# Second attention: score products over all 128 rows, with zero rows for the other head of a pair

## The reference

```python
def _L1_attn_ref(x, Wq, Wk, Wv, Wo, bo, w, v):        # h = 16 heads of hd = 16 channels
    q, k, val = (proj(Wq), proj(Wk), proj(Wv))
    R = jnp.abs(pos[:, None] - pos[None, :]).astype(x.dtype)
    R_hat = (1.0 + jnp.exp(vv)) / (1.0 + jnp.exp(vv - wv * R))
    scores = jax.nn.relu(jnp.einsum('bhqd,bhkd->bhqk', q, k)) * R_hat[None]
    scores = jnp.where(causal[None, None], -jnp.inf, scores)
    attn = jax.nn.softmax(scores / np.sqrt(hd).astype(x.dtype), axis=-1)
    ctx = jnp.einsum('bhqk,bhkd->bhqd', attn, val)
    return ctx @ Wo + bo
```

## Time and profile before

| what | value |
|---|---|
| median of 3 runs | 2512.78 us (2505.85 to 2514.34) |
| the profiled execution | 2507.73 us, its span 2505.9 us |
| TensorE busy over the span | 2114.1 us (84%) |
| VectorE, ScalarE, GpSimd busy | 1612.1, 1338.5, 730.1 us |
| mean granted TensorE clock | 0.916 of full speed |
| L2249, score products | 512, from 1590.8 to 2168.2 us of the span |

### The profile page before, as it was taken

The page is one execution under the profiler, slowest core; times in us unless marked ns, Lnnn a source line. Parts: engine busy times, 40 slices in busy tenths (PEclk is TensorE's granted clock), DMA queues, the critical chain, the costliest instruction groups (busy, mean ns, idle before and its releaser), DMA issues. The chain is left out here.

```text
span 2505.9 us, 43979 instructions
## 1 busy us (share of the span) xinstructions
PE 2114.1 (84%) x13087; PEld 1666.7 (67%) x13087; DVE 1612.1 (64%) x4682; ACT 1338.5 (53%) x2662; POOL 730.1 (29%) x837
## 2 busy tenths in 40 slices
PE   3899999999999999868883685588988889888892
PEld 2788888888888888745562463355655556555782
DVE  4666666666666666356764675787877778676335
ACT  2445555555555544335554664587877778711330
POOL 5211111111111111032455565022222212256452
PEclk8999999999999999979986797699999899989896
DMA  6720010000000000023232433422222222152556
GB/s 110 179 35 5 7 34 1 8 11 27 1 8 3 1 1 0 11 81 59 44 61 55 120 98 128 145 81 79 77 73 59 57 78 83 27 149 103 162 168 240
DMA packets 212265, 167.47 MB, mean 67 GB/s; under 512 B 109185, under 2 KB 170161, under 8 KB 212081
## 3 DMA queue, kind: packets, MB, share of 16 engines
q1 hardware_dynamic: 192608, 121.80, 18.5%
q0 software_dynamic: 14240, 38.35, 4.9%
q10 hardware_dynamic: 5232, 5.14, 0.6%
HBM read 91.07 MB, written 74.14 MB: 66 GB/s over the span
## 5 line engine op out<-in xcount | busy, mean ns | idle before, releaser
L633 PE MATMUL psum_o<-w_s,hid_s 128*128 128x256 f32 x3072 | 384.1, 284 | 19.0 <-ACT hid L437 19.0
L619 PE MATMUL psum_h<-xn2T_s,w_s 128*128 128x512 f32 x1536 | 385.7, 401 | 7.0 <-ACT hid L437 3.7
L633 PEld LDWEIGHTS psum_o<-w_s,hid_s 128*128 128x128 f32 x3072 | 371.8, 188 | 26.9 <-issue 19.0
L436 ACT ACTIVATE hid_s<-psum_h,b 128x512 fp32r<-128x512 f32 x256 | 176.5, 690 | 338.9 <-PE psum_h L619 323.4
L619 PEld LDWEIGHTS psum_h<-xn2T_s,w_s 128*128 128x128 f32 x1536 | 283.3, 190 | 84.4 <-ACT hid L437 21.8
L2134 DVE CUSTOM_DVE_ANT_0 ra_z<-ra_psum_s,rhat 128x128 f32<-128x128 f32 (+3 forms) x512 | 228.6, 483 | 85.3 <-PE ra_psum_s L2249 70.8
L2084 ACT ACTIVATE ra_z<-ra_z,ra_nm 128x128 f32<-128x128 f32 (+3 forms) x512 | 244.7, 555 | 0.0
L2013 POOL TENSOR_SCALAR_AFFINE_SELECT ra_z<-ra_z 128x512 f32<-128x512 f32 x128 | 81.6, 637 | 446.8 <-DVE ra_z L2171 446.8
L2261 PE MATMUL ra_psum_p<-ident,ra_z 128*128 128x128 f32 x1280 | 182.7, 294 | 1.0 <-ACT turned L2076 1.0
L2249 PE MATMUL ra_psum_s<-ra_k_st,ra_q_st 48*128 48x128 f32 (+3 forms) x512 | 126.9, 366 | 63.4 <-DVE ra_mx L2134 47.2
L520 DVE TENSOR_TENSOR hid_s<-hid,hid_s 128x1024 fp32r<-128x1024 f32 x128 | 156.0, 1223 | 35.2 <-ACT hid L437 34.3
(11 more groups left out here) (394 smaller groups left out, 4284.0 us busy)
## 6 DMA issues: line engine op xcount, KB each, us to landing
ex_slots<-blank SPq DMA_DIRECT2D x1, 10296.0 KB, 33.9
ex_zT<-ex_slots SPq DMA_DIRECT2D x78, 132.0 KB
ex_rows<-ex_slots SPq DMA_DIRECT2D x8, 1056.0 KB, 9.8
w<-in_L_tok_w SPq DMA_DIRECT2D x8, 1024.0 KB, 6.4
ra_scratch<-ra_hi SPq DMA_DIRECT2D x32, 256.0 KB
ra_scratch<-ra_lo SPq DMA_DIRECT2D x32, 256.0 KB
ra_q_st<-ra_scratch SPq DMA_DIRECT2D x128, 64.0 KB
ra_k_st<-ra_scratch SPq DMA_DIRECT2D x128, 64.0 KB
```

Of the source, the lines that this page charges most:

```text
L436: act.activation(hid_s[:, 0, m, :], psum_h[:, m % 2, :], ACT.Gelu, bias=b1[:, m:m + 1])
L619: mm = pe.matmul(psum_h[:, m % 2, :], w1_s[:, w_part, k, m * P:(m + 1) * P], xn2T_s[:, x_part, k, :], start=(n == 0 and k == 0), stop=(n = ...
L633: mm = pe.matmul(psum_o[:, t // 2, (t % 2) * D:(t % 2 + 1) * D], hid_s[:, h_part, m, t * P:(t + 1) * P], w2_s[:, w_part, m, :], start=(n = ...
```

## The change

The score products take all 128 rows of `q_st`, both heads of the pair, as weights. `k_st` gets one tile per head: head s finds its keys on its own 48 rows of tile s, and all other rows of that tile stay zero, so the other head's rows of `q_st` are multiplied by zero. `q_st` and `k_st` are cleared once by GpSimd at the stage's start (rows 48 to 63 and 112 to 127 of `q_st` are never loaded), and SyncE waits for both memsets (`st_blank`) ahead of the first load. The loads have the same number and size. To make room, `ctx_all` holds one batch instead of two, which makes its addresses constants.

```diff
-        q_st, k_st = sb("q_st", [P, 2, T], F32R), sb("k_st", [P, 2, T], F32R)
+        q_st, k_st = sb("q_st", [P, 2, T], F32R), sb("k_st", [P, 2, 2, T], F32R)
...
-        ctx_all = sb("ctx_all", [P, 2 * ROW])
+        ctx_all = sb("ctx_all", [P, ROW])
...
-                    for st, qk, parts in ((q_st, 0, ((0, 2, 0), (2, 1, 0))), (k_st, 1, ((0, 1, 0), (1, 2, 0)))):
+                    for st, qk, parts in ((q_st, 0, ((0, 2, 0), (2, 1, 0))), (k_st[:, s, :, :], 1, ((0, 1, 0), (1, 2, 0)))):
...
             store(0, 0)
+            sp.wait_ge(st_blank, 2)
             loads(0, True)
...
             norm.pool_rstd(pool, S.minus_half, 0)
+            pool.memset(q_st[:, :, :].bitcast(F32), 0.0).then_inc(st_blank, 1)
+            pool.memset(k_st[:, :, :, :].bitcast(F32), 0.0).then_inc(st_blank, 1)
...
-                dve.tensor_copy(ctx_now[:, :, :].rearrange("p t c -> p (t c)"), ctx_all[:, ds((b & 1) * ROW, ROW)]).then_inc(ctx_copied, 1)
+                dve.tensor_copy(ctx_now[:, :, :].rearrange("p t c -> p (t c)"), ctx_all[:, :]).then_inc(ctx_copied, 1)
...
-                flat = ctx_all[:, ds((b & 1) * ROW + head * HD + 2 * half * D, D + QUAD * HD)]
+                flat = ctx_all[:, head * HD + 2 * half * D:head * HD + 2 * half * D + D + QUAD * HD]
...
-                        pe.matmul(scores[t], q_st[64 * s:64 * s + 3 * HD, parity, t * P:(t + 1) * P],
-                                  k_st[64 * s:64 * s + 3 * HD, parity, 0:n], start=True, stop=True).then_inc(s_done, 1)
+                        pe.matmul(scores[t], q_st[:, parity, t * P:(t + 1) * P], k_st[:, s, parity, 0:n], start=True, stop=True).then_inc(s_done, 1)
```

More of the change, by code:

```diff
@@ L1914, in relative_attention_stage @@
         inv_ready, ctx_done = sem("inv_ready"), sem("ctx_done")
-        passed, vones = sem("passed"), sem("vones")
+        passed, vones, st_blank = sem("passed"), sem("vones"), sem("st_blank")
         block = ctx.enter_context(nc.Block())
```

## The result

The changed kernel takes **2499.09 us** (median of nine runs, 2493.45 to 2502.91), the kernel before in the same comparison 2512.57 (nine runs, 2499.53 to 2523.01). The ratio is 0.9954, with a 95% interval of 0.9935 to 0.9973: 0.46% faster, 13.5 us. The forecast was 2490 with a range of 2478 to 2504. So the sign and the range hold, and the time lies 9 us above the forecast, just where rival (A) had put it (2499). Whether (A) is the reason is the question of what follows.

The account below looks back on a forecast made before the run. TensorE was taken as the pace in ticks 3 to 13, with waits from tick 14 to 2. 3.2 us per pass times 6 (19.2) plus 2.0 and 1.2 gave 22.4 off 2512.8: 2490 us, range 2478 to 2504.

Parts of the forecast that it names:

- (A): Rival for the score products: loads are not covered, so a head gains only 0.19 us; 2499 us in all; chance 0.18.
- 0.34 us per head: Turned-back transposes to first L2276 product: 0.34 us less per head, 0.09 + 0.09 from two changes, the rest from covered loads.
- The sum of 2.045 us: Forecast time from the first turned-back transpose to the first L2276 product with full-row work, against 2.38 us before.
- The sign that the prediction gave for it: At the score products: the gap ahead goes, but their first weight load starts together with them.
- Ticks 3, 4, 5, 7, 8, 9: In each loop pass, these six ticks gain 0.34 us each, 2.0 us together.
- Tick 6: No L2276 product, and the projection already waits 0.18 us for VectorE: only the 0.2 us ahead of the scores counts.
- Ticks 10 to 12: TensorE would give 1.0 us per pass, but ScalarE has no idle time between exponentials there: 0.5 us taken.
- rival (C): ScalarE as tight in single ticks 3 to 9 as in 10 to 12: whole gain 5 to 7 us, 2506; chance 0.12.
- The turn: Loop stretch from tick 14 to tick 2, where TensorE already waits for VectorE: only 0.15 us counted per pass.
- The memsets, the wait and `ctx_all` at nothing: GpSimd memsets and SyncE's wait are covered by 19 us, and the one-batch context buffer adds no wait: 0 us.
- (D): Rival: longer wait behind tick 14 drops the clock to 1.2 GHz in ticks 14, 15 and 0; 2520 us; chance 0.06.
- Batch 0 and the last batch: Outside the six loop passes: 2.0 us saved in batch 0 and 1.2 us in the last, where ScalarE leaves 1.64.

Follow-up runs that it names:

- both moves: Changed kernel with four of eight scratch stores issued before the loads for ticks 10 and 11, and ScalarE's fill read ahead of its oT copy: 2486.89 us, ratio 0.9894.
- the queue freed: Changed kernel with four of the eight next-batch scratch stores issued ahead of the loads for ticks 10 and 11: ratio 0.9923 to the kernel before.
- without the rows: Changed kernel with score products back on 48 rows, keeping memsets, their wait, second k_st tile and one-batch ctx_all: ratio 1.0004 to the kernel before.

## Why the prediction was right, and where it was not

- **0.34 us per head** held: tick 7 5.20 to 4.86, tick 8 4.78 to 4.44, tick 9 4.78 to 4.44. Of its parts, 0.09 for each change was the smaller half; a change costs 0.17 to 0.19. The forecast that the transposes follow the first score product by 0.63 us was wrong (0.73). The sum of 2.045 us met the measured 2.05 partly by luck: the product of 384 columns was put at 0.175 us and takes 0.23, before and after, while the two transposes and the 128-column product together were put at 0.33 and take 0.28. The saving lies in three places: the score product starts 0.14 us behind the turned-back transposes, where it was 0.31; the transposes follow it 0.10 earlier; and the values follow the transposes after 1.18 us instead of 1.24.
- **(A), only the changes go**, gave the measured time and is wrong. All its ticks would have lost 0.19, and ticks 5, 7, 8, 9 and 13 lost 0.32 to 0.35. The sign that the prediction gave for it (the scores' first load starts with the product) was badly chosen: that load is ahead by 0.03 us only, since the product's recorded start moved with it. Against the last transpose the load has moved by 0.20 us. The rule of the Trainium skill that stood behind it (page "TensorE: Matmul & The Clock Gate", section "Part 3: Packing small matmuls", that a load overlaps only a product of another row group) is not borne out here: the loads of L2263 start 0.22 us ahead of their product behind full-row scores, in the same row group.
- **Ticks 3, 4, 5, 7, 8, 9** held nearly, 1.87 us of 2.04; ticks 3 to 5 gave 0.84 of 1.02.
- **Tick 6 failed**: forecast -0.2, measured +0.5. The prediction had seen the wait of 0.18 us and counted only its own term against it. The step that was missing: what ticks 3 to 5 give up (0.84 us) makes TensorE arrive earlier at the same ScalarE and VectorE work, so the wait grows by about that (from 0.2 to 0.9 us on average). A wait of any length at a stretch's end means that the chain beside it is already the longer one. With both moves tick 6 gives the 0.2.
- **Ticks 10 to 12 failed**: forecast -0.5, measured +0.71. ScalarE's bound was right in itself (with the queue freed they take 0.70 less). What was missing is SyncE's queue, which the prediction did not read in these ticks at all. It is the same mistake as in tick 6: 1.03 us saved in ticks 7 to 9 came back ahead of tick 12, and in batch 1 the low clock added 1.6. Its rival (C), the next engine takes it back, was the right mechanism, but it had been priced for ScalarE in ticks 3 to 9, and it stood in two places and not over all.
- **The turn** gave 0.68 instead of 0.15. The wait in tick 15 grew from 0.64 to 0.79 us, about as expected (0.9), as the row below shows. Most of the difference is in tick 2, which took 4.91 to 5.28 us before, 4.08 to 4.80 after and 4.68 to 4.80 in the version with both moves, where the turn gives 0.19. The granted clock is below full speed here, and where in the tick it rises again differs from pass to pass; why it lay favourably after is open. Where the clock is 0.50 all through the tick, it takes 5.28 us before and 4.80 after.

```profile
1882.60 0.41 PE L2239 MATMUL ra_psum_s<-ident,ra_oT 128*128 128x128 f32 x2 [0.79 <-DVE ra_mx L2137]
```

- **The memsets, the wait and `ctx_all` at nothing** held (1.0004 without the rows). **(D), the clock**, did not come where it was expected: the clock from tick 14 to tick 2 is 0.80 against 0.81. But its mechanism, a longer wait and a lower clock behind it, did come in tick 12 of batches 0 and 1, at about 1.5 us each.
- **Batch 0 and the last batch**: forecast 2.0 and 1.2. The last gave 1.4 (51.9 to 50.5 us). Batch 0 gave 0.1 (77.4 to 77.3): it waits 1.41 us for its load of tick 12, which it did not before, loses 1.5 in that tick to the clock, and gets 1.8 back in tick 15, where the clock is at 1.00 instead of 0.66. With the queue freed the batch takes 74.5.

So the stage gave 11.5 us (576.9 to 565.4) where 22.4 were forecast, and the runs 13.5; the missing 11 us are in the main the two waits (13.2 us more by the tables) and the low clock behind one of them (3 us), less what the turn and tick 15 of batch 0 gave beyond the forecast. With both moves it gives 24.1. The mechanism and the size per head were right; the sum failed by adding savings over ticks without asking, at each point where TensorE meets another queue, how much lead that queue had. That the time still fell inside the range, 9 us from the forecast, owes something to luck: two stretches went the other way, and the turn and the clock in tick 15 of batch 0 gave some 5 us that were not forecast.

## What to carry to other kernels

When a saving recurs in every step of a pipeline, don't multiply it by the steps: find each meeting point with another queue (DMA issue, copy-out, reduction), take the time from one meeting to the next on both sides, and cap the gain at the other side's slack. Here it was half a microsecond at most in a chain of 21, and it showed before as a wait in one batch only, since a queue that is just in time shows none. A new wait can also lower the clock of the work behind it; here that cost as much again as the wait. And where small-row products alternate with full-array ones, zero rows that make them all alike can pay: here they were worth 0.17 us per change, with the columns the same.

## What the runs showed of the hardware

- The cost lies in the change between 48 or 64 rows and all 128: 48 and 64 rows are the same (0.83 and 0.84 us from scores to transposes), 112 and 128 are the same (0.73). Between 64 and 112 nothing was run.
- Two more changes inside one group of four products cost 0.39 us (0.19 each), a little more than those at its borders.
- SyncE issues a load of 64 KB and one of 32 KB in 0.78 us together, but a 256 KB store takes 0.61 to 1.44 us of issue, and the first pair of loads behind eight stores 1.69 to 2.55 us. Eight stores hold the queue for 9 us.
- Behind a new wait of 1.41 and 1.78 us the granted clock was 0.60 and 0.71 in the tick that followed, and a tick of 4.35 us at full clock took 5.96; without the wait it was 1.00.
